# Four chained programs of an attention and feed-forward layer become one block with single waits, together with a rebuilt projection and the causal mask moved from TensorE to VectorE

## What is computed

```python
q = split_heads(x @ Wq.T + bq); k = split_heads(x @ Wk.T + bk); v = split_heads(x @ Wv.T + bv)
q, k = rope(q), rope(k)                 # Y * cos + turned(Y) * sin, 16 heads of 16
att = einsum('bhqd,bhkd->bhqk', q, k) / sqrt(16)
att = softmax(where(tril, att, -inf))
x = layernorm(x + (att @ v) @ Wo.T + bo)
h = silu((x @ w1.T) * w1_s) * ((x @ w2.T) * w2_s)      # hidden width 1024
h = gelu((h @ h1.T) * h1_s)
h = gelu((h @ h2.T) * h2_s)
x = layernorm(x + (h @ w3.T) * w3_s)
```

## Time and profile before

| | |
|---|---|
| median of 3 runs | 2890.32 us (2888.95 to 2891.99) |
| the profiled execution | 2888.47 us |
| its span, first to last instruction | 2886.7 us |
| TensorE busy | 2781.7 us, 96% |
| VectorE busy | 1944.8 us, 67% |
| ScalarE busy | 1296.6 us, 45% |
| GpSimd busy | 94.8 us, 3% |
| mean granted TensorE clock | 0.984 |

### The profile page before, as it was taken

How to read it: one execution, slowest core, us unless ns; L and a number is a source line. 1 busy time by engine, 2 the same in 40 slices (tenths; PEclk the granted TensorE clock), 3 DMA queues, 4 the chain that set the end, 5 groups by cost and what they waited for, 6 DMA issues and landing times. The chain is left out here.

```text
span 2886.7 us, 39857 instructions
## 1 busy us (share of the span) xinstructions
PE 2781.7 (96%) x15456; PEld 1474.2 (51%) x15456; DVE 1944.8 (67%) x3592; ACT 1296.6 (45%) x2545; POOL 94.8 (3%) x121
## 2 busy tenths in 40 slices
PE   8949999999999999999999999899999999999998
PEld 4423333333333333333333333388888887888887
DVE  7979999988888887888887776353333333344343
ACT  0005666677776676777777777511112111101100
POOL 0030100002000010000000000000000000000000
PEclk9969999999999999999999999999999999999999
DMA  5540270008000017000001000221111132112100
GB/s 155 166 106 27 45 89 3 3 2 103 7 3 4 5 28 91 3 3 3 3 3 38 18 4 8 75 71 56 57 59 64 48 124 111 44 44 87 44 15 23
DMA packets 94569, 132.89 MB, mean 46 GB/s; under 512 B 30688, under 2 KB 68192, under 8 KB 90688
## 3 DMA queue, kind: packets, MB, share of 16 engines
q1 hardware_dynamic: 83184, 96.91, 10.4%
q0 software_dynamic: 5472, 23.34, 6.5%
q10 hardware_dynamic: 5744, 10.36, 1.2%
HBM read 83.25 MB, written 47.32 MB: 45 GB/s over the span
## 5 line engine op out<-in xcount | busy, mean ns | idle before, releaser
L531 DVE TENSOR_REDUCE at_segmax<-at_row 128x1 f32<-128x512 f32 (+3 forms) x2304 | 1329.1, 638 | 236.2 <-PE at_row L454 178.3
L595 ACT ACTIVATE at_probs<-at_key 128x512 f32<-128x512 f32 (+3 forms) x2304 | 1130.9, 567 | 532.6 <-PE at_key L470 362.3
L454 PE MATMUL at_row<-fr_k_stack,fr_q_stack 96*128 96x512 bf16 (+3 forms) x1152 | 407.3, 374 | 32.2 <-POOL at_values L367 28.3
L470 PE MATMUL at_key<-fr_q_stack,fr_k_stack 99*128 99x512 bf16 (+3 forms) x1152 | 414.7, 364 | 2.7 <-ACT at_probs L595 2.7
L454 PE MATMUL at_row<-at_k_stack,at_q_stack 96*128 96x512 bf16 (+3 forms) x1152 | 412.1, 364 | 1.4 <-DVE at_segmax L531 1.2
L470 PE MATMUL at_key<-at_q_stack,at_k_stack 99*128 99x512 bf16 (+3 forms) x1152 | 402.8, 364 | 6.7 <-ACT at_probs L595 6.2
L489 PE MATMUL at_o<-at_probs,at_values 128*32 128x512 f32 (+3 forms) x2304 | 286.9, 570 | 0.0
L489 PE MATMUL at_o<-at_probs,fr_values 128*32 128x512 f32 (+3 forms) x2304 | 286.4, 569 | 0.0
L454 PEld LDWEIGHTS at_row<-fr_k_stack,fr_q_stack 96*128 96x128 bf16 x1152 | 112.1, 99 | 309.2 <-DVE at_segmax L531 202.1
L454 PEld LDWEIGHTS at_row<-at_k_stack,at_q_stack 96*128 96x128 bf16 x1152 | 112.0, 97 | 293.2 <-DVE at_segmax L531 211.1
L1128 ACT ACTIVATE na_h3f<-na_h,na_hs 128x512 f32<-128x512 f32 x64 | 44.1, 690 | 401.9 <-PE na_h L1098 401.9
(11 more groups left out here) (125 smaller groups left out, 2702.7 us busy)
## 6 DMA issues: line engine op xcount, KB each, us to landing
hidden<-wi_h SPq DMA_DIRECT2D x64, 256.0 KB, 2.0
na_h2f<-hidden SPq DMA_DIRECT2D x8, 1024.0 KB, 8.4
q_parts<-pr_parts SPq DMA_DIRECT2D x48, 128.0 KB, 1.9
k_parts<-pr_parts SPq DMA_DIRECT2D x48, 128.0 KB, 2.2
at_q_stack<-q_parts POOLq DMA_DIRECT2D x48, 128.0 KB, 23.8
at_k_stack<-k_parts POOLq DMA_DIRECT2D x12, 512.0 KB, 27.7
values<-pr_vals SPq DMA_DIRECT2D x32, 136.0 KB, 2.8
outputs<-at_outs SPq DMA_DIRECT2D x128, 34.0 KB
```

The lines of the kernel that those rows point to most:

```text
L454: last = nc.tensor.matmul(bank[:, 0:w], qst[u][0:SROWS, c, h, i * P:(i + 1) * P], kst[u][0:SROWS, h, s * CH:s * CH + w], start=True, stop= ...
L470: last = nc.tensor.matmul(bank[:, q0:CH], kst[u][0:SROWS + PARTS, h, j * P:(j + 1) * P], qst[u][0:SROWS + PARTS, c, h, q0:CH], start=True, ...
L531: nc.vector.tensor_reduce(segmax[:, n % 2, h * TPC + i, s:s + 1], row_ps[r % RING_R][:, 0:w], op=ALU.max, axis=AX.X).then_inc(rows_taken, 1)
L595: nc.scalar.activation(probs[:, g % RING_P, h, q0:CH], key_ps[m % RING_K][:, q0:CH], ACT.Exp).then_inc(probs_ready, 1)
```

## The change

Four edits are joined.

1. **Projection.** One product per unit; ScalarE adds the bias and scales it into SBUF (`pr_lin`), TensorE turns that by one matmul with a constant 128x128 matrix (`turn`), GpSimd multiplies with cosine (`t1`), VectorE with sine (`t2`). ScalarE makes the first two bf16 parts, VectorE the rest. VectorE has four 128x512 instructions per unit instead of seven. There are three buffers of input, four of parts, and the loops are written out. SyncE's queue loads the first x chunk.
2. **Hand-over to attention.** ScalarE's queue loads the stacks of chunks 0 to 2 of quad 0 in the middle of the projection (12 DMAs each). The constant rows of ones come by DMA from a new input; both memsets of 3x16384 are gone.
3. **Diagonal.** TensorE's mask matmul in the row units is gone. VectorE reads the diagonal scores and a constant `causal` by one tensor_tensor_reduce (add, then max), followed by an instruction that reads the accumulator.
4. **One block.** The three barriers are gone; where a stage takes over buffers, one of its engines waits for the last semaphores of the stage ahead.

```diff
@@ project
+            def main(g):
+                ...
+                for c in range(DH):
+                    last = nc.tensor.matmul(main_ps[g % 3][:, :], w[m // DH][:, c, cols], xt[:, n % BUFS, c, :],
+                                            start=(c == 0), stop=(c == DH - 1))
+                last.then_inc(main_ready, 1)
+            def rotate(g):
+                ...
+                if g >= 2:
+                    pe.wait_ge(t2_ready, g - 1)
+                pe.wait_ge(lin_ready, g + 1)
+                nc.tensor.matmul(rot_ps[g % 2][:, :], turn[:, :], lin[:, g % 3, :], start=True, stop=True).then_inc(rot_ready, 1)
+            main(0)
+            for g in range(NU):
+                if g + 1 < NU:
+                    main(g + 1)
+                rotate(g)
+                if g % 2 == 1:
+                    values(g // UNITS, g % UNITS // 2)
@@ project, scalar
+            linear(0)
+            for g in range(NU + 1):
+                if g + 1 < NU:
+                    linear(g + 1)
+                if g < NU:
+                    act.wait_ge(full_ready, g + 1)
+                    ...
+                    nc.scalar.activation(parts[:, g % SLOTS, 0, :], full[:, g % 2, :], ACT.Copy).then_inc(hi_ready, 1)
+                if g >= 1:
+                    act.wait_ge(rest_ready, g)
+                    nc.scalar.activation(parts[:, (g - 1) % SLOTS, 1, :], rest[:, (g - 1) % 2, :], ACT.Copy
+                                         ).then_inc(mid_ready, 1)
+                ...
+                if m == 3 and 2 <= n < 2 + FIRST_EARLY:
+                    for slot in range(SLOTS):
+                        act.wait_ge(parts_stored[slot], 16 * PARTS * (n - 1))
+                    front.load_first(act, qp_d, kp_d, n - 2)
@@ project, gpsimd
+                nc.gpsimd.tensor_tensor(t1[:, g % 2, :], lin[:, g % 3, :], cos[:, n % BUFS, :], ALU.mult
+                                        ).then_inc(t1_ready, 1)
@@ attend, gpsimd
+            for i in range(2):
+                pool.wait_ge(*projected[f"v_stored{i}"])
             load_values(0, 0)
-            for u in range(2):
-                nc.gpsimd.memset(vq[u][:, NT * QUAD * VW:], 0.0).then_inc(pad_ready, 1)
-                pool.wait_ge(pad_ready, u + 1)
-                nc.gpsimd.memset(kst[u][SROWS:SROWS + PARTS, :, :], 1.0).then_inc(ones_ready[u], 1)
-                pool.wait_ge(ones_ready[u], 1)
@@ attend, tensor
-                                        kst[u][0:SROWS, h, s * CH:s * CH + w], start=True, stop=(s < c))
-                if s == c:
-                    last = nc.tensor.matmul(bank[:, w - P:w], mask[:, :], ident[:, :], start=False, stop=True)
+                                        kst[u][0:SROWS, h, s * CH:s * CH + w], start=True, stop=True)
                 last.then_inc(rows_ready, 1)
 ...
+            for name in ("lin_ready", "t2_ready", "v_taken"):
+                pe.wait_ge(*projected[name])
@@ attend, vector
+                if s == blocks[n][1]:
+                    if diagonal[r] >= 2:
+                        dve.wait_ge(rows_taken, diagonal_at[diagonal[r] - 2] + 1)
+                    nc.vector.tensor_tensor_reduce(out=masked[:, diagonal[r] % 2, 0:w], in0=row_ps[r % RING_R][:, 0:w], in1=causal[:, CH - w:CH],
+                                                   scale=1.0, scalar=MASKED, op0=ALU.add, op1=ALU.max,
+                                                   accum_out=segmax[:, n % 2, h * TPC + i, s:s + 1]).then_inc(rows_taken, 1)
+                    return
@@ widen
+            sp.wait_ge(*attended["probs_used"])
+            for i in range(2):
+                sp.wait_ge(*attended[f"out_stored{i}"])
 ...
+            pe.wait_ge(prep.w_split, 4)
+            for name in ("probs_ready", "out_taken"):
+                pe.wait_ge(*attended[name])
@@ narrow
+            pe.wait_ge(*widened["hid_taken"])
 ...
+            dve.wait_ge(*widened["hid_ready"])
             split_h2(0, 0)
@@ build
-        project(nc, io, qp_d, kp_d, v_d)
-        attend(nc, io, qp_d, kp_d, v_d, max_d, o_d, front, prep)
-        widen(nc, io, h2_d, front, prep)
-        narrow(nc, io, x1_d, h2_d, out, front)
+        block = ctx.enter_context(nc.Block())
+        projected = project(nc, block, ctx, io, qp_d, kp_d, v_d, front)
+        attended = attend(nc, block, ctx, io, qp_d, kp_d, v_d, max_d, o_d, front, prep, projected)
+        widened = widen(nc, block, ctx, io, h2_d, front, prep, attended)
+        narrow(nc, block, ctx, io, x1_d, h2_d, out, front, widened)
```

More of the change, by code:

```diff
@@ L48 @@
 SLACK = 28 * CH
-FIRST_AHEAD = 3
+FIRST_EARLY = 3
+FIRST_AHEAD = 4
 RING_R = 4
@@ L299, in attend @@
     out_after = {min(g + 1, NG - 1): n for n, g in last_group.items()}
+    diagonal_at = [r for r, (n, i, _, s) in enumerate(rows) if i != TURN and s == blocks[n][1]]
+    diagonal = {r: k for k, r in enumerate(diagonal_at)}
     MR = PARTS * QUAD * TPC
@@ L434, in _ @@
             prep.store_x1(sp, 0)
-            for i in range(2):
-                sp.wait_ge(out_stored[i], 16 * QUAD * (NB // 2))
         @block.tensor
```

379 lines of the change are left out of this document (206 added, 173 removed).

## The result

| | kernel before | changed kernel |
|---|---|---|
| median | 2889.64 us (2888.95 to 2891.99, 4 runs) | 2836.78 us (2832.43 to 2839.76, 4 runs) |
| the profiled execution | 2888.47 us | 2839.76 us |
| its span | 2886.7 us | 2837.9 us |

The ratio is 0.9815, with a 95% interval of 0.9801 to 0.9828: the change is worth 1.9%, about 53 us. The forecast was 2818, a gain of 72.8; the time lies inside the range, but 19 us above the forecast. It also lies above the forecast's own part of the range, 2803 to 2832. It happens to be the 2837 us of rival B, and it will turn out that rival B is not the reason.

What follows compares the result with a forecast made beforehand. VectorE was taken to bound the projection and early attention, TensorE attention from 546 us. Terms -46.5 - 6.4 + 13.0 - 18 - 10.8 - 4.1 = -72.8 us gave 2815.7, on the median's scale 2818; range 2790 to 2850.

Steps and rivals of the forecast that it cites:

- rival B: Projection: VectorE and GpSimd hold each other up for whole instructions, 4.2 us a unit, 19.2 us later, 2837; chance 0.20.
- Faster, and mainly through the projection and the seam behind it: Start to attention's first row unit: 142.8 instead of 189.3 us, -46.5 us, at 3.6 us a unit; faster overall 0.94.
- the bursts: Projection: ScalarE issues 12 loads in a row in three chunks, about 4 us lost each time, 12 in all.
- The load of the values: Start of attention: it waits for the projection's last store, but the first key unit stands near 28 us later, so hidden.
- The second memset: Start of attention: GpSimd's second memset held a VectorE cast for 6.39 us and the row units behind it; gone, -6.4 us.
- Diagonal on VectorE: Attention's row units: the masked reduction costs 0.15 us extra per diagonal; quad 0 +13.0 us net, hidden in quads 1 to 3.
- rival C: Attention's diagonal: the masked reduction runs at half rate, 0.49 us extra, total 2873; chance 0.07.
- D: Attention: the masked reduction makes VectorE the bound throughout; at 0.8 us extra 2979, decides from about 0.62; chance 0.05.
- Diagonal on TensorE: Attention, quads 1 to 3: 384 mask matmuls at 0.055 us saved, 21 us, of which -18 us was counted.
- Attention to widen: Handover ahead of widen: TensorE's gap shrinks by 8.2 us and the low clock's 2.6 go, together -10.8 us.
- Widen to narrow: Handover ahead of narrow: VectorE's first split starts with TensorE's end near 2419.1 instead of 2423.28, -4.1 us.
- The prediction's own sign of being wrong: Projection: prediction wrong if GpSimd's product takes over 2 us or VectorE's sums stretch beside it.

Runs made afterwards that it cites:

- e2_pad_late: Changed kernel, but TensorE waits for the zeros behind quad 1's values only ahead of quad 1's first values product; median 2831.45 us.
- e5_mask_matmul: Changed kernel with the row units' diagonal as before: mask matmul on TensorE, plain maximum on VectorE; median 2852.01 us.
- e1_ahead3: Changed kernel with FIRST_AHEAD, the blocks SyncE's queue loads stacks ahead in quad 0, put back from 4 to 3; median 2822.97 us.
- e7_bulk_late: Changed kernel with FIRST_AHEAD kept at 4, but GpSimd's load of quad 1 waits until block 4's maxima are reloaded; median 2823.86 us.
- e4_direct: Changed kernel, but VectorE's first split of narrow waits for its input's load itself, not for SyncE's signal behind the last stores; median 2831.27 us.
- e3_w3_behind: Changed kernel, but the 1 MB load of w3 is issued by SyncE behind the last stores of h2 instead of by ScalarE; median 2835.05 us.

## Why the prediction was right or wrong

- **Faster, and mainly through the projection and the seam behind it**: right, -40.4 us for -46.5. The sum down to VectorE's end came out, 140.8 for 142.8, with terms off in both directions. A unit takes 3.44 us and not 3.6 (the chain of five engines costs nothing in the steady state, -5 us); the bursts cost 12.3 for 12, and some 3.5 us more by the low clock behind two of them (0.62 and 0.61 granted for 4.3 and 4.4 us). The first sine product came at 12.61 for 13.1, partly by luck: TensorE began at 5.43 and not at 7.2, and a table load of 1.28 us on ScalarE ahead of its first linear step, which the sum lacks, took most of that back. The failed step is the one that sets the first row unit equal to VectorE's end: "Behind the last unit VectorE has 2.5 us of sums and splits. First row unit: 13.1 + 115.2 + 12 + 2.5 = 142.8". The 2.5 held (2.3 are left of 140.8 when the terms above are taken off), but TensorE started at 148.88, held by a wait of GpSimd's; without that wait it starts 8.0 us earlier, at 140.91 (`e2_pad_late`).
- **"The load of the values now waits for the projection's last store ... so it is hidden"** was right about the load and blind to what stands behind it: a memset queued after that load, and TensorE's wait for it. The order of GpSimd's queue was in the code.
- **The second memset**: -6.0 for -6.4, as read.
- **Diagonal on VectorE, 0.15 us each, +13.0 us**: wrong, it is nothing (`e5_mask_matmul`). The failed step is the choice of 0.15 from durations (690, 682 and 158 ns): the accumulator read overlaps, and the masked reductions stand 0.61 us apart, the plain ones 0.60. The page "Vector Engine (DVE) Microarchitecture Reference" of the Trainium skill, cited for rival C, speaks of two SBUF sources; with one in PSUM the trace shows no such cost, and rivals C and D, which needed 0.49 and 0.62 us extra, fall with it.
- **Diagonal on TensorE, -18 us** in quads 1 to 3: 12 to 17 by the same run, 11.8 in the ledger. The mechanism holds; the term was up to a third too high (a mask matmul cost the path 0.03 to 0.045 us, not 0.055).
- **FIRST_AHEAD** has no term in the sum. It made +14.2 us, as large an error as the diagonal's and of the other sign (`e1_ahead3`, `e7_bulk_late`). The parameter looks like an earlier load of small pieces; what it moved is the big load that waits for the last piece, from where its delay is covered to where it isn't.
- **Attention to widen, -10.8**: -10.5, right in size. Its cause is only in part the barrier: 2.1 us of gap and 1.5 to 2.5 by the clock; 6.2 are the stores' landing, now off TensorE's path.
- **Widen to narrow, "VectorE's first split can start with TensorE's end near 2419.1 ... -4.1 us"**: failed, +3.6. VectorE waits for a signal that stands behind a store in SyncE's order (`e4_direct`), and the load that the barrier had held back makes that store slow (`e3_w3_behind`). TensorE's idle time, 1.3 expected, is 2.40 with the first of these removed.
- **Rival B** gave the measured time by another road. Its hold is real, its 4.2 us a unit are not: the holds are 0.62 us a unit on the mean and not 1.2, and the instructions start 0.60 us apart and not 0.65, so VectorE needs 4 x 0.60 + 0.33 + 0.62 = 3.35 us, just under TensorE's 3.44 (it is busy 24.73 of 25 us from 105 to 130). Had B been judged by the time alone, it would have passed for proven. The prediction's own sign of being wrong, that "VectorE's sums stretch beside it", did come true without any cost to the path: a stretched instruction off the path is no such sign.
- **The tail**, +3.2 us behind the last store, was not foreseen. All eleven profiles with one block show it (6.5 to 6.6 us from the issue of the last store to the end of the span; 3.3 to 3.4 in the three with barriers). What the engines do there the trace doesn't show, and no run was made for it: it stays open.

## What to carry to other kernels

When barriers go, list for each single wait what stands ahead of the signal in the order of the engine that gives it: two of the four losses here (zeros behind a load, a signal behind a store) were of that kind. List also the bulk loads that now start earlier: in the other two losses one of them met a transfer on the path (w3, which a barrier had held back, the last store of h2; the big load, moved by FIRST_AHEAD, the maxima). Here a small DMA that the compute waits for was late by what was left of the bulk load it met; compare that with the work standing ahead of the wait, and a look-ahead parameter is to be followed to everything that waits for its last piece. Moving work from VectorE to GpSimd was worth only what is left after the holds, here nothing; read the pair's durations beside each other before counting the relief.
